# Unpacking, projections and the first gate/up products put elsewhere in an attention and feed-forward kernel

## The reference, cut to what matters

```
x (16, 128, 512), ctx (16, 128, 512); 8 heads of 16 channels each, 512 positions
q = Wq @ layernorm(x) + bq;  k = Wk @ ctx + bk;  v = Wv @ ctx + bv      # per batch
q, k = rope(q), rope(k)                                                 # half of a head's channels
out = softmax(q k^T / 4) v                                              # per head, 512 x 512
x = x + tanh(g_xattn) * (Wo @ out + bo)
w_gu (2816, 512), w_down (512, 1408) = fp4 codes * a scale per group of 128 inputs
gate, up = split(layernorm(x) @ w_gu^T)
y = (silu(gate) * up) @ w_down^T
x = x + tanh(g_ffn) * y / sqrt(mean(y^2) + 1e-6)
```

## Time and profile before

| | |
|---|---|
| time, median of 3 runs | 728.29 us (728.08 to 728.73) |
| the profiled execution | 727.19 us |
| its span in the profile | 725.4 us |
| PE busy | 689.1 us (95%) |
| DVE busy | 611.1 us (84%) |
| ACT busy | 521.4 us (72%) |
| POOL busy | 476.5 us (66%) |
| granted PE clock, mean | 0.973 |

### The profile page before, as it was taken

One profiled execution on the slowest core, in us unless ns is written; L12 is line 12 of the kernel. 1 busy time (PEld: TensorE's weight loads), 2 busy tenths in 40 slices (PEclk: granted clock), 3 DMA queues, 4 the chain that ended last, 5 costly groups with the idle time before them and its releaser, 6 DMA issues.

```text
span 725.4 us, 13353 instructions
## 1 busy us (share of the span) xinstructions
PE 689.1 (95%) x4660; PEld 334.3 (46%) x4660; DVE 611.1 (84%) x825; ACT 521.4 (72%) x925; POOL 476.5 (66%) x403
## 2 busy tenths in 40 slices
PE   3579999999999999999999999999999999999995
PEld 1234434443444344434443444656565556555653
DVE  6599989888988898888889779766899789977894
ACT  2028888888888888888888876665666566666653
POOL 2946555786678667866633129876697669766773
PEclk9559999999999999999999999999999999999999
DMA  6877777787777877877663202000001000100011
GB/s 206 219 184 168 180 197 190 175 184 205 201 173 178 216 184 182 201 197 190 166 150 70 85 24 74 1 1 0 1 1 44 15 1 0 45 16 0 4 42 72
DMA packets 48935, 80.59 MB, mean 111 GB/s; under 512 B 14436, under 2 KB 17892, under 8 KB 48868
## 3 DMA queue, kind: packets, MB, share of 16 engines
q1 hardware_dynamic: 47568, 78.73, 42.6%
q10 hardware_dynamic: 1300, 1.01, 0.5%
HBM read 45.11 MB, written 32.24 MB: 107 GB/s over the span
## 4 chain that ended last, share of the span: by engine, by line
PE 52%; POOL 26%; issue 14%; DVE 4%; DMA 2%; ACT 1%; SPq 0%; POOLq 0%; ACTq 0%; DVEq 0%
PE pv_ps L845 20%; POOL probs L300 15%; PE s_ps L815 14%; PE st_ps L827 9%; POOL probs L304 9%; DVE max_rows L1113 2%; PE st_ps L800 2%; PE st_ps L857 2%; PE st_ps L788 2%; PE st_ps L794 2%; POOL over_stack L224 1%; DMA xt_all<-x_dram 1%; DMA image<-split_rest 1%; DMA qk_stack<-image 1%; ACT probs L950 0%
## 5 line engine op out<-in xcount | busy, mean ns | idle before, releaser
L1113 DVE TENSOR_REDUCE max_rows<-s_ps 128x2 f32<-128x1024 f32 x256 | 305.2, 1212 | 44.9 <-PE s_ps L815 44.1
L950 ACT ACTIVATE probs<-st_ps 128x512 f32<-128x512 f32 x512 | 277.6, 596 | 63.8 <-PE st_ps L827 53.0
L319 ACT ACTIVATE probs<-s_ps,gu_sc 128x512 f32<-128x512 f32 x176 | 117.7, 685 | 84.4 <-PE s_ps L405 84.2
L300 POOL TENSOR_TENSOR probs<-probs 128x512 f32<-128x512 f32 x88 | 120.3, 1371 | 69.4 <-ACT probs L319 69.0
L845 PE MATMUL pv_ps<-probs,v_all 128*32 128x256 f32 x2048 | 163.2, 391 | 2.2 <-ACT pv_all L956 2.2
L815 PE MATMUL s_ps<-qk_stack 48*128 48x512 f32 x512 | 133.7, 519 | 8.4 <-DVE max_rows L1113 7.4
L171 DVE SCALAR_TENSOR_TENSOR proj<-s_ps,gu_sc,proj 128x512 f32<-128x512 f32 x132 | 98.7, 748 | 11.1 <-PE s_ps L405 1.9
L827 PE MATMUL st_ps<-qk_stack 50*128 50x512 f32 x512 | 108.0, 411 | 0.0
L421 PE MATMUL st_ps<-dn_head,over_input 128*128 128x512 f32 x264 | 104.9, 423 | 1.0 <-DVE over_input L182 1.0
L815 PEld LDWEIGHTS s_ps<-qk_stack 48*128 48x128 f32 x512 | 49.7, 191 | 115.8 <-issue 71.7
L845 PEld LDWEIGHTS pv_ps<-probs,v_all 128*32 128x32 f32 x2048 | 40.6, 108 | 97.8 <-ACT probs L950 81.3
(11 more groups left out here) (120 smaller groups left out, 883.6 us busy)
## 6 DMA issues: line engine op xcount, KB each, us to landing
qk_stack<-image SPq DMA_DIRECT2D x60, 384.0 KB, 6.2
image<-split_head SPq DMA_DIRECT2D x31, 256.0 KB
image<-split_head SPq DMA_DIRECT2D x62, 128.0 KB
image<-split_rest SPq DMA_DIRECT2D x31, 256.0 KB
xt_all<-x_dram SPq DMA_DIRECT2D x16, 256.0 KB, 4.0
ct<-ctx_dram SPq DMA_DIRECT2D x16, 256.0 KB, 3.4
scale_of<-inverse_scratch SPq DMA_DIRECT2D x16, 256.0 KB
out_dram<-over_stack SPq DMA_DIRECT2D x16, 256.0 KB, 2.0
```

The source lines that it names most:

```text
L300: nc.gpsimd.tensor_tensor(pair[:, n], parts[T_ % 2][:, 2 * n], parts[T_ % 2][:, 2 * n + 1], ALU.add).then_inc(pairs_ok, 1)
L319: nc.scalar.activation(parts[T_ % 2][:, k], gu_ps[(2 * k) % BANKS], ACT.Copy, scale=gu_sc[:, k, T_ % IT:T_ % IT + 1]).then_inc(gate_read, 1)
L950: nc.scalar.activation(probs[at % PROBS][:, tile % 4, :], st_ps[item % ST_BANKS][:], ACT.Exp).then_inc(st_read, 1)
L1113: nc.vector.tensor_reduce(out, s_ps[item % S_BANKS][:], AXIS_X, ALU.max).then_inc(s_read, 1)
```

## The change

The edits fall in three places. **First stage:** PE begins with 9 products of a tile of ones into `pv_ps`; batches 1 and 2 are both projected ahead of the scores; v of batch 0 goes behind the score of slot 3, the tiny products behind slots 5 and 6. DVE rotates batch 0 right after its normalising, then does batches 1 and 2, batch 3's statistics and the two conversions of the gate/up scales, all ahead of the maxima. SP stores the second half's rest addend (`store_rest(sp, 0, 1)`), ACT's queue only the heads, now ahead of batch 1's bias. **Unpacking:** the codes are loaded one batch earlier, and DVE unpacks one piece in batch 13's and one in batch 14's step, after slots 2, 5 and 11. **Where the blocks meet:** the inputs are turned in slots 9 to 12; products 0 to 5 of step 0 are made in slots 13 to 15, 6 and 7 right behind them and ahead of the last values; DVE takes the gate parts of step 0 as well as the up parts, into `xn` instead of the first `probs` tile; `vector_step` and `scalar_step` take nothing for step 0 any more; POOL adds them once all values are done, and its `invert_dev(0)` goes ahead of `residual(13)`.

```
-SCALE_AT, DN_AT, GU_AT = 2, 3, 10
+SCALE_AT, DN_AT, GU_AT = 2, 3, 9
+WORDS_AT = (2, 5, 11)
-FIRST_TURN, TAIL_AT = 12, 3
+FIRST_TURN, TAIL_AT, WARM = 9, 3, 9
+FIRST_UP = (13, 14, 15)
...
+    def first_takes(dve):
+        for k in range(KT):
+            dve.wait_ge(gate_done, k + 1)
+            if k == 0:
+                dve.wait_ge(turned, KT)
+            nc.vector.tensor_scalar(xn[:, k], gu_ps[(2 * k) % BANKS], gu_sc[:, k, 0:1], None, ALU.mult).then_inc(gate_read, 1)
+            take_up(dve, 0, k)
...
     def pool_step(pool, T_):
+        part = parts[T_ % 2] if T_ else xn
+        if T_ == 0:
+            pool.wait_ge(keep["pv_done"], B * SPANS)
...
     def take_gate(act, T_, k):
+        if T_ == 1 and k == 0:
+            act.wait_ge(gate_read, KT)
...
                 store_projection(sp, 0, 0)
+                store_rest(sp, 0, 1)
...
+                    if b == B - 1 and slot in FIRST_UP:
+                        if slot == FIRST_UP[0]:
+                            pe.wait_ge(gu_turned, 2 * BIT_STEPS)
+                        for n in (2 * FIRST_UP.index(slot), 2 * FIRST_UP.index(slot) + 1):
+                            ffn["gate_up"](pe, 0, n)
...
+                pe.wait_ge(values_set, 1)
+                for _ in range(WARM):
+                    nc.tensor.matmul(pv_ps[:, 0:P], ones[:, 0:P], ones[:, 0:P], start=True, stop=True)
                 pe.wait_ge(weights_in, WEIGHTS)
                 project_rot(pe, 0)
                 project_pass(pe, 0)
-                project_rot(pe, 1)
-                project_pass(pe, 1)
-                pe.wait_ge(wv_in, 16)
-                project_v(pe, 0)
-                project_rot(pe, 2)
-                project_pass(pe, 2)
-                nc.tensor.matmul(pv_ps[:, 0:1], wo[:], bias_v[:], start=True, stop=True).then_inc(spread, 1)
-                nc.tensor.matmul(pv_ps[:, 2:4], ones_row[:], gate_in[:], start=True, stop=True).then_inc(spread, 1)
+                for n in (1, 2):
+                    project_rot(pe, n)
+                    project_pass(pe, n)
                 for slot in range(SLOTS):
                     score(pe, 0, slot)
+                    if slot == 3:
+                        project_v(pe, 0)
+                    if slot == 5:
+                        pe.wait_ge(wo_in, 16 * 4)
+                        nc.tensor.matmul(pv_ps[:, 0:1], wo[:], bias_v[:], start=True, stop=True).then_inc(spread, 1)
+                    if slot == 6:
+                        pe.wait_ge(gates_in, 32)
+                        pe.wait_ge(consts, 5)
+                        nc.tensor.matmul(pv_ps[:, 2:4], ones_row[:], gate_in[:], start=True, stop=True).then_inc(spread, 1)
                 for b in range(B):
                     tensor_step(pe, b)
-                pe.wait_ge(gu_turned, BIT_STEPS)
-                for n in two:
+                for n in (2 * KT - 2, 2 * KT - 1):
                     ffn["gate_up"](pe, 0, n)
...
-                    if n == 2:
-                        take_v(act, 0)
-                        store_projection(act, 0, 1)
+                    if n == 1:
+                        store_head(act, 0, 1)
...
+                take_v(act, 0)
...
+                    if slot in WORDS_AT and b >= B - 3:
+                        piece = b - (B - 3)
+                        dve.wait_ge(gu_in[piece], 16 * 4)
+                        turn_nibbles(dve, gu_bits, WORDS_AT.index(slot), slice(piece * DN_WORDS, (piece + 1) * DN_WORDS),
+                                     BIT_STEPS * piece, gu_turned)
...
-                statistics(dve, 1)
-                normalise(dve, nc.vector, 1)
                 rotate_first(dve)
-                statistics(dve, 2)
-                normalise(dve, nc.vector, 2)
+                for n in (1, 2):
+                    statistics(dve, n)
+                    normalise(dve, nc.vector, n)
+                statistics(dve, 3)
+                dve.wait_ge(scales_in, 16)
+                nc.vector.tensor_scalar(keep["gu_sc"][:, :, 0:IT], gu_sc16[:, :, 0:IT], 4.0 / X_GAIN, None, ALU.mult).then_inc(scales_ok, 1)
+                nc.vector.tensor_scalar(keep["gu_sc"][:, :, IT:GU], gu_sc16[:, :, IT:GU], 16.0 / X_GAIN, None, ALU.mult).then_inc(scales_ok, 1)
...
-                turn_gate_up(dve, 0)
...
-                turn_gate_up(dve, 1)
...
+                ffn["first_takes"](dve)
...
+                ffn["invert_dev"](pool, 0)
                 residual(pool, nc.gpsimd, B - 3)
-                ffn["invert_dev"](pool, 0)
```

More of the change, by code:

```diff
@@ L76, in transposed_items @@
     for n in range(AHEAD_PROJ):
-        if n == 2:
-            items.append(("v", 0))
         items += [("rot", n), ("pass", n)]
+    items.append(("v", 0))
     for b in range(B):
@@ L260, in vector_step @@
         drains = T_ < NT and g > 0 and t == EVAC_AT
-        if T_ < NT:
+        if 0 < T_ < NT:
             take_up(dve, T_, 0)
@@ L299, in pool_step @@
                 pool.wait_ge(gate_ok, T_)
-            nc.gpsimd.tensor_tensor(pair[:, n], parts[T_ % 2][:, 2 * n], parts[T_ % 2][:, 2 * n + 1], ALU.add).then_inc(pairs_ok, 1)
+            nc.gpsimd.tensor_tensor(pair[:, n], part[:, 2 * n], part[:, 2 * n + 1], ALU.add).then_inc(pairs_ok, 1)
         pool.wait_ge(pairs_ok, 2 * T_ + 2)
@@ L429, in feed_forward @@
             "last_squares": last_squares, "statistics": statistics, "normalise": normalise, "input_rest": input_rest,
-            "first_input_head": first_input_head, "vector_step": vector_step, "last_finish": last_finish,
+            "first_input_head": first_input_head, "first_takes": first_takes, "vector_step": vector_step, "last_finish": last_finish,
             "invert_dev": invert_dev, "pool_step": pool_step, "last_root": last_root}
@@ L491, in attend @@
         scales_in = sem("scales_in")
-        gu_in = sem("gu_in")
+        gu_in = [sem(f"gu_in{p}") for p in two]
         dn_in = sem("dn_in")
@@ L531, in attend @@
         max_in = [[sem(f"max_in{p}{h}") for h in two] for p in two]
-        pv_done = sem("pv_done")
+        pv_done = keep["pv_done"]
         pv_out = [sem(f"pv_out{h}") for h in two]
@@ L732, in load_gate_up @@
                     words = gu_bits[halves[half], :].rearrange("c (k w) -> c k w", k=KT)[:, k]
-                    sp.dma_start(words, rows).then_inc(gu_in, 16)
+                    sp.dma_start(words, rows).then_inc(gu_in[k // 2], 16)
             @block.sync
@@ L881, in tensor_step @@
                         ffn["turn_inputs"](pe, 0, slot - FIRST_TURN)
+                    if b == B - 1 and slot in FIRST_UP:
[3 more added lines that the diff above has]
+                            ffn["gate_up"](pe, 0, n)
             def tensor_feed(pe, T_):
                 g, t = divmod(T_, IT)
-                if T_ < NT:
-                    for n in range(2 if T_ == 0 else 0, 2 * KT):
-                        if T_ == 0 and n == KT:
-                            pe.wait_ge(gu_turned, 2 * BIT_STEPS)
+                if 0 < T_ < NT:
+                    for n in range(2 * KT):
                         if T_ == TAIL_AT + 1 and n == 0:
@@ L906, in _ @@
             def _(pe):
+                pe.wait_ge(values_set, 1)
+                ones = v_ones[0].rearrange("p k j q c -> p (k j q c)")
+                for _ in range(WARM):
+                    nc.tensor.matmul(pv_ps[:, 0:P], ones[:, 0:P], ones[:, 0:P], start=True, stop=True)
                 pe.wait_ge(weights_in, WEIGHTS)
@@ L1163, in vector_step @@
                         turn_nibbles(dve, dn_bits, slot - (SLOTS - BIT_STEPS), slice(t * T // 4, (t + 1) * T // 4), BIT_STEPS * t, dn_turned)
-            def turn_gate_up(dve, piece):
-                for step in range(BIT_STEPS):
-                    turn_nibbles(dve, gu_bits, step, slice(piece * DN_WORDS, (piece + 1) * DN_WORDS), BIT_STEPS * piece, gu_turned)
             @block.vector
@@ L1182, in _ @@
                 nc.vector.memset(ones_row[:], 1.0).then_inc(consts, 1)
-                statistics(dve, 1)
-                normalise(dve, nc.vector, 1)
                 dve.wait_ge(table_in, TABLES)
                 rotate_first(dve)
-                statistics(dve, 2)
-                normalise(dve, nc.vector, 2)
+                for n in (1, 2):
[5 more added lines that the diff above has]
+                nc.vector.tensor_scalar(keep["gu_sc"][:, :, IT:GU], gu_sc16[:, :, IT:GU], 16.0 / X_GAIN, None, ALU.mult).then_inc(scales_ok, 1)
                 for slot in range(SLOTS):
                     maxima(dve, 0, slot)
-                    if slot == 1:
-                        statistics(dve, 3)
                     if slot == 7:
@@ L1203, in _ @@
                 turn_max(dve, B - 1, 1)
-                dve.wait_ge(gu_in, 32 * KT)
-                turn_gate_up(dve, 0)
                 for j in range(GROUP):
@@ L1293, in build @@
             "x_ok": ctx.enter_context(nc.semaphore("x_ok")),
+            "pv_done": ctx.enter_context(nc.semaphore("pv_done")),
             "gates": sb("gates", [P, 2], F32),
```

7 lines of the change are left out of this document (1 added, 6 removed).

## The result

| | kernel before | changed kernel |
|---|---|---|
| median | 728.22 us (726.43 to 728.99, 9 runs) | 730.56 us (729.07 to 731.54, 9 runs) |
| profiled execution; span | 727.19; 725.4 us | 729.35; 727.5 us |

The ratio of the times is 1.0036, with an interval of 1.0025 to 1.0046: the change costs 2.6 us (1.8 to 3.4), more than the 0.2% that a measurement can tell from no change. The forecast of 728.8 stood for "no change"; the time lies in the range, on the slower side.

A forecast was written before the change was run, and what follows sets the result against it. PE was taken to bound nearly all of the run; -1.3 + 0.3 + 1.5 = +0.5 us on the profiled 727.19 gave 727.7, and the median, 1.1 above, 728.8; range 725.6 to 731.4.

The forecast's parts named there:

- First stage, -1.3: Start of the kernel: earlier rotation, maxima and reload make PE's step 0 1.3 us earlier (0 to -2.0).
- DVE's hole of 1.6 for v: Start, first maxima: DVE stands 1.6 us while PE makes batch 0's v, taken as 2.3 us cold.
- Unpacking, +0.3: Steps of batches 13 and 14: PE waits 0.15 us in each for DVE's unpacking, +0.3 us (0 to 2.6).
- rival C: Batches 13, 14 and slot 9's turning: DVE and POOL delay each other, +2.3 us, 731.1; chance 0.14.
- Meeting, +1.5: Where the blocks meet: later values delay group 1's load and step 2's product 5, +1.5 us (-0.8 to +2.0).
- Now some 1.9 us later: Meeting: batch 15's values end at 432.6 instead of 430.67, from 2.6 us of added products less filled holes.
- the hole of 0.57: PE's idle 0.57 us between 417.96 and 421.97, which the earlier turnings were to fill.
- So PE's product 5 of step 2 comes 1.9 - 0.43 = 1.5 us later: Meeting, step 2: DVE's statistics wait for the later load ahead of `take_up`, whatever PE won before; 1.5 us later.
- Rival A: Whole kernel: the main forecast as summed, 728.8 us, no change; chance 0.40.
- Rival B: Start: PE's clock rises during the projections and stays up, winning 2.2 us, 726.6, faster; chance 0.27.
- Rival D: Start: nothing is won, as the reload waits for crowded stores; 730.1, slower; chance 0.11.
- step 0 near 46.5: Sign for right, at the start: PE's step 0 begins near 46.5 us, against 47.80 before.

The follow-up runs named there:

- the statistics later: Changed kernel with DVE taking the statistics of group 1's first batch in step 2 instead of step 1; 726.88 us, 0.9988 of the kernel before.
- the load ahead with the sums later: Changed kernel with group 1's load issued before batch 15's gather and merge, and the last reciprocal behind step 1; 726.66 us, 0.9991 of the kernel before.
- the change with the new order: Changed kernel with group 1's four statistics at the ends of steps 2, 3, 4 and 4; 725.97 us, 0.9984 of the kernel before.
- the load ahead: Changed kernel with SP issuing group 1's load before the gathering and merging of batch 15; 730.44 us, 1.0051 of the kernel before.
- the load ahead and the statistics later: Changed kernel with group 1's load issued before batch 15's gather and merge, and its first statistics in step 2; 729.80 us, 1.0047 of the kernel before.

## Why the prediction was right or wrong

- **First stage, -1.3: right in sum**, 1.39 in the trace and 1.2 in the medians, but not in its steps. The rotation began at 8.48 (9.2 forecast): the warm projection ended earlier, where I had taken ACT's bias as unmoved. First maxima at 26.72 against 27.0. DVE's hole of 1.6 for v was 0.40: the clock, at 0.50 there in the kernel before, was at 1.00 for some 3 us, and v took 1.4 instead of 2.3:

```profile
27.00:30.00 3.00, 1.45 (x9) 0.81 (x8) 3.00 (x3) 0.00 (x0) 2.85 (x3) 1.00 1.05 199
30.00:33.00 3.00, 2.70 (x13) 1.75 (x11) 2.60 (x4) 0.60 (x1) 2.86 (x4) 0.55 0.82 225
```

  So the ninth maximum came at 36.96, not 38.3; the reload then at 38.61 (39.1 forecast), 1.8 earlier than before, and step 0 2.26 earlier. The clock's rise, 8.7 us behind step 0 instead of 6.7, took 0.87 of it back. That the sum came out is in part luck: the cold clock that the prediction had for v was off one way, its rise behind step 0, which the prediction took as unmoved, the other.
- **Unpacking, +0.3: right within its bounds.** No step grew in the profile of the change; the part alone was 0.8 slower, by a meeting of DVE and POOL. Over the eleven traces with the unpacking in the steps, the stretch between first values that holds batch 13's piece grew by 0 to 0.55 us, and that with batch 14's by 0 to 0.98: at most 1.0 and in the mean 0.3 for both. So rival C had the mechanism right, and made its largest size the rule.
- **Meeting, +1.5: mis-sized; it was +3.56.** Two things were off. The wait: 1.95 net of what PE had won, against 1.5. "Now some 1.9 us later" for the end of the values was 2.48 (431.76 against 430.67 less the lead of 1.39). Three things add up to the difference. Four products cost 0.97 us with what stands between them and the next work, where the sum had 0.86: 0.2 in all. Of the hole of 0.57 that was to be filled 0.17 stayed. And DVE's four normalisings took 2.79 us beside POOL's `residual`, where 1.92 stood before, which held PE's turning at slot 9 for 0.2 (it began 0.77 behind the start of the values ahead of it, where other work follows such values by 0.57); rival C had named this meeting. The normalisings before, then those after with PE's rows:

```profile
418.31 1.92 DVE L224 TENSOR_SCALAR over_stack<-over_stack,neg_mean_ffn,rstd_ffn 128x512 f32<-128x512 f32 x4 [3.63 <-POOL rstd_ffn L201]
```

```profile
415.00 2.79 DVE L233 TENSOR_SCALAR over_stack<-over_stack,neg_mean_ffn,rstd_ffn 128x512 f32<-128x512 f32 x4 [1.61 <-POOL rstd_ffn L210]
...
417.17 0.64 PE L860 MATMUL pv_ps<-probs,v_all 128*32 128x256 f32 x8
...
417.94 0.63 PE L402 MATMUL s_ps<-ident,over_stack 128*128 128x128 f32 x4
```

  And the step that failed, "So PE's product 5 of step 2 comes 1.9 - 0.43 = 1.5 us later", ended the account there: with PE 0.8 us early ahead of it, it had the hole of PE grow from 1.29 us to more than 3, and asked only when the next product starts, not at what clock it runs. That is the 1.61 us that make the result "slower" instead of "no change". The time is in the range all the same, but not by this account: the slow end had been set by rival C, whose meetings of DVE and POOL cost little here.
- **Rival A** named the right mechanism and the right chain to the last link (values, gather, merge, load, statistics, `take_up`); the statistics later and the load ahead with the sums later both take it away. **Rival B** (the clock stays up at the start) did not come: 0.51 from 48 to 54.3. The clock mattered at the other end. **Rival D** did not come.
- The two trace signs that I gave for "right" came (first maxima near 27.0; product 5 waiting over 2 us behind statistics that wait for a DMA); the hole of 1.6 and step 0 near 46.5 did not. Of the signs for "wrong" one came, a clock of 1.00 before 50 us, for some 3 us from 27 on.

## What to carry to other kernels

When an edit lets one engine run ahead, look for the next wait on a transfer that hangs on the work that you put in front: here 2.6 us of products moved ahead of the last values made the next 1 MB load 2.5 us later, and DVE, in order, held PE's own work for it. Cost a hole of PE by its length and, where it is near the 3 us and more of these traces, by a possible fall of the clock behind it; products in the hole, useful or not, kept the clock. And move the waiting instruction (a statistic, a reciprocal) behind the work that doesn't need it before you move the transfer: here the small transfer behind the large one on the same queue landed with it (the load at 438.9, the gather at 439.1).

The best kernels measured are the first stage with the statistics at the ends of steps 2, 3, 4 and 4 (0.9978), the first stage alone (0.9983) and the change with the new order (0.9984); between them the intervals don't decide.

## What was not expected of the hardware

- A hole of 3.11 us in PE, mid-kernel, was followed by about 3.3 us of products at half clock (0.63 us each instead of 0.38 to 0.40), 1.6 us lost. Holes of 3.26 (the change without its first stage) and 3.14 us (without the ones) did the same, and 4.07 us with the load ahead; one of 3.79 us, with the load ahead and the statistics later, did not, in its one profile. So a hole of this length is not followed by the lower clock each time; what decides, no run here settles. Holes of 1.29 to 1.48 us at the same place did not.
- The rise of the clock at the start came 6.7 to 10.4 us behind the first product of step 0, in kernels whose work there is nearly the same. From step 0 to the first values of batch 14 the fourteen profiles have 340.92 to 342.63 us, 1.7 us of scatter.
- An 8 KB gather took 5.6 us to land when issued 0.6 us behind a 1 MB load, and 1.8 us ahead of it.
- A `tensor_scalar` of DVE on SBUF (64x1408 words) took 0.87 to 1.96 us for the same shape beside a two-input instruction of POOL, which took 1.27 to 2.04.
